# A four-layer graph kernel: the fp32r copy of the adjacency by a converting DMA of GpSimd in place of a ScalarE pass, with new orders

## Time and profile before

| | |
|---|---|
| median of three runs | 1117.52 us |
| the profiled execution, its own time | 1112.79 us |
| its span, first to last instruction | 1110.8 us |
| mean granted TensorE clock | 0.962 |
| HBM read / written | 38.61 MB / 4.19 MB |

### The profile page before, as it was taken

The page is one execution under the profiler, slowest core; times in us unless marked ns, Lnnn a source line. Parts: engine busy times, 40 slices in busy tenths (PEclk is TensorE's granted clock), DMA queues, the critical chain, the costliest instruction groups (busy, mean ns, idle before and its releaser), DMA issues.

```text
span 1110.8 us, 16047 instructions
## 1 busy us (share of the span) xinstructions
PE 961.9 (87%) x5024; PEld 616.0 (55%) x5024; DVE 945.3 (85%) x2710; ACT 885.8 (80%) x1876; POOL 97.7 (9%) x138
## 2 busy tenths in 40 slices
PE   4577897998989898998989898998989899898875
PEld 3354565656556565656556565656556565655442
DVE  4387889899898989989898999989898998988543
ACT  2378797979989797988989797988979798787643
POOL 1101010100101011010101010010101101000000
PEclk7569999999999999999999999999999999999989
DMA  2021102011111202011110201111110201101000
GB/s 88 10 76 48 39 11 86 11 39 49 48 48 35 61 11 70 27 39 48 48 48 10 86 11 44 43 48 49 48 48 10 85 2 40 48 1 48 1 10 9
DMA packets 34028, 43.92 MB, mean 40 GB/s; under 512 B 1040, under 2 KB 17424, under 8 KB 33936
## 3 DMA queue, kind: packets, MB, share of 16 engines
q1 hardware_dynamic: 25488, 38.61, 11.0%
q10 hardware_dynamic: 8448, 4.20, 1.3%
HBM read 38.61 MB, written 4.19 MB: 39 GB/s over the span
## 4 chain that ended last, share of the span: by engine, by line
PE 50%; DVE 32%; ACT 8%; issue 6%; POOL 3%; DMA 0%; DVEq 0%; ACTq 0%; POOLq 0%
DVE probs L604 8%; PE l_bank L865 7%; PE x_bank L949 5%; PE a_bank L894 5%; DVE probs L618 4%; DVE sess L774 3%; PE r_bank L1010 3%; DVE sess L767 3%; PE n_bank L1023 3%; ACT hn L368 3%; PE n_bank L1026 3%; PE a_bank L865 3%; PE n_bank L1010 2%; PE h_bank L1013 2%; PE l_bank L915 2%
## 5 line engine op out<-in xcount | busy, mean ns | idle before, releaser
L618 DVE SCALAR_TENSOR_TENSOR probs<-spread,s_lift,probs 128x512 f32<-128x512 f32 x320 | 232.9, 747 | 1.8
L604 DVE CUSTOM_DVE_ANT_0 probs<-spread,mask 128x512 f32<-128x512 f32 x320 | 211.9, 684 | 4.1 <-ACT spread L428 4.1
L444 ACT ACTIVATE pT<-l_bank 128x512 f32<-128x512 f32 x256 | 153.6, 600 | 40.7 <-PE l_bank L865 40.7
L436 ACT ACTIVATE probs<-probs,shift_p 128x512 f32<-128x512 f32 x256 | 184.7, 722 | 1.5 <-DVE probs L618 1.5
L865 PEld LDWEIGHTS l_bank<-ident,probs 128*128 128x128 f32 x1024 | 124.5, 144 | 79.0 <-issue 40.6
L865 PE MATMUL l_bank<-ident,probs 128*128 128x128 f32 x1024 | 155.9, 278 | 10.1 <-ACT probs L436 9.4
L350 POOL TENSOR_TENSOR rstd<-var_eps,power 128x4 f32<-128x4 f32 x64 | 74.1, 1158 | 967.1 <-DVE var_eps L598 641.6
L368 ACT ACTIVATE hn<-x,shift,rstd 128x128 f32<-128x128 f32 x192 | 79.4, 497 | 34.4 <-POOL shift L352 34.4
L915 PE MATMUL l_bank<-hT,dst_rep 128*128 128x512 f32 x128 | 71.9, 645 | 12.9 <-ACT pT L444 11.0
L428 ACT ACTIVATE spread<-l_bank 128x512 f32<-128x512 f32 x64 | 38.3, 599 | 41.9 <-PE l_bank L915 41.9
L996 PE MATMUL y_bank<-hn,sess 128*128 128x128 f32 x512 | 64.3, 279 | 8.2 <-DVE sess L774 8.2
(11 more groups left out here) (174 smaller groups left out, 2017.7 us busy)
## 6 DMA issues: line engine op xcount, KB each, us to landing
adj_i<-in_adj SPq DMA_DIRECT2D x16, 1024.0 KB, 5.1
adjt_i<-in_adj_t SPq DMA_DIRECT2D x16, 1024.0 KB, 5.5
xin<-in_x SPq DMA_DIRECT2D x16, 256.0 KB, 2.8
out<-out_sb ACTq DMA_DIRECT2D x16, 256.0 KB, 4.7
weights_sb<-in_weights SPq DMA_DIRECT2D x1, 840.0 KB, 4.4
```

Of the source, the lines that this page charges most:

```text
L436: s.activation(row, row, ACT.Exp, bias=shift_p[:, head, c:c + 1], accum_out=den[:, head, c:c + 1]).then_inc(probs_ready, 1)
L444: s.activation(pT[:, head - 1, :, c * P:(c + 1) * P], l_banks[unit % 2][:, :].rearrange("p (j i) -> p j i", j=C), ACT.Copy).then_inc(pT_co ...
L604: chain.link(v.tensor_tensor_reduce(out=row, in0=spread_row, in1=mask, scale=1.0 / LIFT, scalar=-3e38, op0=ALU.subtract, op1=ALU.max, accu ...
L618: v.scalar_tensor_tensor(row, spread_row, source, row, ALU.min, ALU.subtract, reverse1=True).then_inc(ready, 1)
```

## The change

The step edges is taken off ScalarE and put on GpSimd. There it is a DMA that reads adj (int32) from HBM again and writes it as fp32r into edges, with a semaphore for each buffer. The one user in the common case, TensorE's first agg of a graph, waits for the DMA's semaphore of its buffer. (VectorE's kinds step, in the way that is not taken here, then makes the values 0 or 1.) SyncE's load of the next adj_i no longer waits for edges. All of BEGIN and WHEN is replaced.

```diff
@@ BEGIN, WHEN: every number of the two tables is new @@
 BEGIN = (
-    (-21509, 8739, 15282, 21773, 28348, 34972, 41515, 48098, 54718, 61258, 67837, 74403, 80989, 87504, 94130,
-     100679),
...
+    (-5429, 20041, 26606, 33143, 39707, 46288, 52827, 59483, 66019, 72571, 79073, 85623, 92241, 98809, 105411,
+     111896),
...
@@ graph_layers @@
-        mask1_ready, count_ready, edges_ready = sem("mask1_ready"), sem("count_ready"), sem("edges_ready")
+        mask1_ready, count_ready = sem("mask1_ready"), sem("count_ready")
+        edges_loaded = [sem("edges_loaded0"), sem("edges_loaded1")]
@@ SyncE, load_adj @@
                     sp.wait_ge(mask1_ready, p.before().count(1, 1))
                     sp.wait_ge(count_ready, p.before().count(1, 1))
-                    sp.wait_ge(edges_ready, p.before().count(1, 1))
                 sp.dma_start(adj_i[:], rows(adj, p.graph)).then_inc(adj_loaded, 16)
@@ GpSimd, step_of @@
             def step_of(p, step):
+                if step == "edges":
+                    if p.before(2).exists():
+                        pool.wait_ge(agg_ready, p.before(2).count(LAYERS, LAYERS))
+                    g.dma_start(edges[:, p.graph % 2, :, :], rows(adj, p.graph)).then_inc(edges_loaded[p.graph % 2], 16)
                 if step[:5] == "stats":
                     deviation(p, int(step[5]))
@@ ScalarE, step_l @@
-                elif step == "edges":
-                    act.wait_ge(adj_loaded, p.count(16, 16))
-                    if p.before(2).exists():
-                        act.wait_ge(agg_ready, p.before(2).count(LAYERS, LAYERS))
-                    s.activation(edges[:, p.graph % 2, :, :], adj_i[:, :, :], ACT.Sign).then_inc(edges_ready, 1)
@@ VectorE, kinds (the way not taken) @@
-                        dve.wait_ge(edges_ready, p.count(1, 1))
+                        dve.wait_ge(edges_loaded[par], p.count_of_parity(16, 16))
@@ TensorE, agg @@
                     if layer == 0:
-                        pe.wait_ge(edges_ready, p.count(1, 1))
+                        pe.wait_ge(edges_loaded[par], p.count_of_parity(16, 16))
```

More of the change, by code:

```diff
@@ L41 @@
 BEGIN = (
-    (-21509, 8739, 15282, 21773, 28348, 34972, 41515, 48098, 54718, 61258, 67837, 74403, 80989, 87504, 94130,
-     100679),
[L44 to L49, removed]
+    (-5429, 20041, 26606, 33143, 39707, 46288, 52827, 59483, 66019, 72571, 79073, 85623, 92241, 98809, 105411,
+     111896),
+    (13526, 20049, 26553, 33166, 39703, 46305, 52896, 59433, 66037, 72495, 79063, 85666, 92240, 98820, 105362,
+     111953),
+    (13568, 20072, 26599, 33185, 39754, 46342, 52950, 59490, 66040, 72590, 79193, 85741, 92297, 98872, 105445,
+     112031),
+    (13546, 20068, 26667, 33223, 39788, 46390, 52950, 59524, 66016, 72579, 79189, 85731, 92330, 98847, 105476,
+     112046),
 )
```

## The result

The change took 1113.13 us (median of 20 runs, 1110.89 to 1117.25) against 1117.74 us (20 runs, 1112.52 to 1121.01): a ratio of 0.9967, with a 95% interval of 0.9954 to 0.9980. It is faster by 0.3%, some 4 us, where 11.1 us were forecast. The direction held and the size did not.

What follows compares the result with a forecast made beforehand. One loop was taken to bound it: VectorE from x2 to stats3, normalisation, TensorE from agg to x2. Over 12 periods at 0.8 us, -9.6, plus -1.5 filling, gave -11.1: 1106.4 us from 1117.5; own range 1097 to 1114, 8-in-10 range 1092 to 1123.

Steps and rivals of the forecast that it cites:

- The pass: ScalarE's edges pass, 1.900 us a graph, 30.4 us in all: off the loop, its removal costed at nothing in steady state.
- The issue: GpSimd's issue of each edges DMA, 0.37 to 2.41 us, between stats2 and stats3: hidden by idle time, costed at 0.
- the rival in which it keeps VectorE out: GpSimd's issue behind stats2 stops VectorE 1.01 or 2.41 us a graph: slower, 1122.6 to 1145.0 us; chance 0.13.
- VectorE's waits around x2: Waits for z_t and state_hi get smaller, a new one of 1 to 2 us for y_bank comes at x2.
- the filling of the pipeline: While the pipeline fills, the edges pass is on the chain; removing it gives -1.5 us.
- the term of x2: VectorE's x2 starts earlier, with mask1 filling the z_t wait and the state_hi wait gone: mean -1.15 us a period.
- g1_turn and src0: These VectorE steps now lie between x2 and stats3, costing 0.61 and 0.07 us: +0.68 us a period.
- values0 ahead of norm3: ScalarE does values0 in the 1.37 us it waited before norm3, bringing the split nearer: -0.40 us a period.
- First failed step: the clock: Periods at 0.97 take 64.3 and 64.6 us instead of 63.1; more or fewer move the time 1.3 us each, within range.
- The draining: The pipeline's end keeps its order of TensorE and VectorE work but for a few places: 0.
- It costs no more work (1.22 us either way), but fills the 1.09 us wait for z_t.: VectorE's mask1 ahead of g1_joint_r instead of behind mix; its price is n_t, count and avT 0.26 us later.
- Nothing gained: Removed waits come back elsewhere in the loop, both full engines keeping their work: 1117.5 us; chance 0.15.

Runs made afterwards that it cites:

- experiment 4: The kernel before with its old orders, edges by GpSimd's DMA in place of ScalarE's pass: 1116.74 us, 0.9999 (0.9975 to 1.0023).
- experiment 3: The changed kernel with the edges DMA issued for the first two graphs alone, later graphs reusing their adjacency: 1115.83 us, 0.9985 (0.9965 to 1.0006).
- experiment 9: The kernel before with one filling matmul, its result unread, ahead of rows3 on TensorE: 1109.83 us, 0.9955 (0.9934 to 0.9976).
- experiment 10: The changed kernel with two filling matmuls, their results unread, ahead of rows3 on TensorE: 1103.68 us, 0.9873 (0.9838 to 0.9907).
- experiment 1: The changed kernel with VectorE's src0 put back behind stats3: 1112.5 us, 0.9965 (0.9947 to 0.9983).
- 7: The kernel before with one move, mask1 directly behind stats1 on VectorE, no DMA on GpSimd: 1127.14 us, 1.0106 (1.0079 to 1.0134).
- 11: The changed kernel with mask1 behind the next graph's stats0 and two filling matmuls ahead of rows3: 1095.92 us, 0.9819 (0.9789 to 0.9849).
- experiment 12: The kernel of 11 with VectorE's max2 and src0 ahead of m0 behind stats3, and n7 ahead of x3: 1105.9 us, 0.9897 (0.9868 to 0.9926).

## Why the prediction was wrong in size

**What held.** The pass is worth nothing in steady state (experiment 4: 0.9999). The issue (0.81 us) and the landing (5.7 us) of the DMA cost nothing (experiment 3, and no wait of TensorE for edges). The issue lay between the 0.37 and 2.41 us given, and the rival in which it keeps VectorE out has no trace in 746 ns. The Trainium skill (DMA: Bandwidth & Descriptors, Anatomy of one DMA) gave an estimate of 4.4 us for the landing; the trace has 5.5 to 6.1 us for this converting transfer, so it takes a good microsecond longer than by that fit, to no effect here. VectorE's waits around x2 changed as said. For the filling of the pipeline, forecast at -1.5 us, experiments 9 and 10 have -1.2 us, but this shows nothing: up to the first split the profiled executions take 124.3 to 130.5 us, as the clock happens to be, so a term of this size can't be told.

Periods at full clock were forecast shorter by 0.87 us, taken as 0.8, and the pair of experiments 9 and 10 has 0.62 (62.48 against 63.10 us). That this is near was luck. The terms of the sum can be read in these two kernels (means of twelve graphs; x2 is its first instruction on VectorE, stats3 its var_eps, and the twelve graphs give 0.65 us a period):

| stretch and term | forecast | experiment 9 | experiment 10 | change |
|---|---|---|---|---|
| agg to the next x2: the term of x2 | -1.15 | 33.23 | 33.19 | -0.04 |
| x2 to stats3: g1_turn and src0 | +0.68 | 25.04 | 24.84 | -0.20 |
| stats3 to agg: values0 ahead of norm3 | -0.40 | 4.92 | 4.52 | -0.40 |

values0's term was right, with the mechanism given (norm3 no later, the split 0.4 us nearer). The term of x2 came to nothing, and the price of g1_turn and src0 was not paid: VectorE's busy time in that stretch grew by less than 0.1 us, so other steps had left it, which I had not looked for. Two errors cancelled.

**First failed step: the clock.** The sentence was: "More or fewer of them move the time by 1.3 us each, and this is in the range." I treated the clock as chance that both kernels share. It is not: it hangs on TensorE's waits at rows3, which the new orders changed. I had counted src0 ("+0.68", with g1_turn) as a cost of time alone. With s_lift ready earlier, values0's matmuls no longer wait, and two waits of TensorE of 1.43 us became one of 2.45 us. Nine periods of twelve have a clock of 0.97 in after's profile, two in before's. That the filling removes the falls is shown; that the joined wait makes them more frequent than the split one is likely but not shown, since experiment 1 did not split it, and the split waits of experiments 4 and 7 had falls in six and eight periods of twelve. Over the same thirteen graphs, filling TensorE's wait gives before 824.29 - 820.28 = 4.0 us and after 824.48 - 812.18 = 12.3 us, in the profiled runs. The two stretches without filling, of before and then of after:

```profile
192.02:1016.31 824.29, 749.85 (x4046) 481.86 (x4044) 755.58 (x2149) 710.62 (x1515) 75.26 (x102) 0.99 0.13 40
```

```profile
193.96:1018.44 824.48, 763.77 (x4047) 490.65 (x4047) 752.39 (x2152) 692.83 (x1502) 93.74 (x115) 0.98 0.19 57
```

The difference, 8.3 us, is as much as the 8.1 us that the new orders are worth there. By the medians it is milder, because before's other runs lose more than its profiled one and after's less: filling brings before 0.45% (5 us) and after 0.9% (10 us). So the clock took some 5 us of the forecast 11, and where it did not act, the change is worth 6 us (medians) to 9 us (ratios).

The draining was put at 0, and that failed by the same step: behind the last but one split, before's profile takes 56.03 us with a clock of 0.96 to the last split, after's 58.60 us with 0.91, and from there to the end they take 38.5 and 38.4 us. That is 2.5 us more.

**Second failed step: the term of x2, and mask1 in it.** The sentence was: "It costs no more work (1.22 us either way), but fills the 1.09 us wait for z_t." It costs VectorE nothing and GpSimd 0.9 us, on the path over norm1 to n_t, count and avT, which I had named myself as what is late next. I had avT 0.26 us later. Counted from agg, avT starts 0.78 us later (30.90 us behind it in experiment 9, 31.68 in 10), and 0.34 us later with mask1 moved (31.24 in 11; means of twelve graphs). From avT's start to x2 I had 1.25 us, and it is 1.51 us. TensorE did lose work from this stretch, as forecast, but it now spends the time won waiting for avT; of the whole change this was the rival "Nothing gained", and for this term it held. One such stretch, agg to x2, of the kernels of 9 and of 10; the second and third columns are its length and TensorE's busy time:

```profile
381.89:415.29 33.40, 33.33 (x191) 21.16 (x191) 30.21 (x81) 31.68 (x71) 2.78 (x4) 1.00 0.03 9
```

```profile
378.83:412.14 33.31, 32.59 (x187) 20.72 (x188) 29.93 (x82) 31.88 (x72) 3.69 (x4) 1.00 0.05 10
```

So -1.15 us was mis-sized by 1.1 us, of which mask1's place is 0.43 (with it moved, the stretch takes 32.76 us, -0.47). Moving mask1 is worth 0.44 us a period (experiments 10 and 11), 4 to 8 us in all. The Trainium skill (SBUF — State Buffer, Who interferes with whom) says that a VectorE operation that can enter a 2-port mode shuts GpSimd out for the whole instruction when it comes first, and that one with two SBUF inputs contends with GpSimd's reads. The runs agree in this case: mask1 began 0.17 us ahead and the rstd ended 0.9 us late, and the rstd beside m0 took 1.40 us, though the shift behind it got shorter by as much or more. The rule has two sides, and I used one. I priced GpSimd shutting out VectorE, and took VectorE's steady 740 to 753 ns as evidence that the two do not meet. The evidence was in the other engine's row: the longest rstd of before, 2.41 us beside a median of 1.007, stood in the earlier trace rows, and I used it as a bound and not as a sign; mask1 runs within it (156.77 to 157.99 us, the rstd from 155.62 to 158.03 us). Before even had the very pair while its pipeline filled, GpSimd first:

```profile
48.89 1.91 POOL L350 TENSOR_TENSOR rstd<-var_eps,power 128x4 f32<-128x4 f32 x1 [0.17 <-DVE var_eps L598]
...
48.72 1.22 DVE L670 TENSOR_SCALAR mask<-adj_i 128x2048 bf16<-128x2048 int32 x1
```

**Left open.** What about TensorE's waits brings the clock down was not measured beyond these cases: in after nine of twelve waits of 1.95 to 2.72 us had a fall behind them, and one of 2.39 us had none; the waits of 1.91 to 2.03 us in experiment 1 had one in seven cases of twelve; two waits with 1.6 us of matmuls between them (631.52 to 633.11 in before) had one in two, six and eight cases of twelve in before and experiments 4 and 7. The length of the wait does not decide alone. In experiment 9 only the wait for hn was filled and that for s_lift stayed (12.7 us in 11 cases, at most 1.4, in 205 to 900 us), and still the falls behind rows3 went. Why mask1's early place brings more falls in before was not settled either. No kernel was tried with mask1 at a place where GpSimd has nothing to do.

## What to carry to other kernels

When orders are changed, list the waits of TensorE by length and not by sum: a wait costs more than its length where the clock falls behind it, and a few matmuls without use in the gap are a cheap test for it (here they also pay). Check every term of a sum by its own stretch, since a total can be near by luck. When a large VectorE pass is moved, look at what GpSimd does at its new place; a GpSimd operation of 128 x 4 on the path to the next stage can wait for nearly all of it, and this is seen in GpSimd's durations, min, median and max, never in VectorE's. Look also at the operation behind it: a shorter rstd here only made the shift longer. Compare kernels by the same periods of the same graphs before summing up; here the three that kept the full clock were the short ones anyway.

## What the runs showed of the hardware

- An int32 to bf16 pass of VectorE (128 x 2048, 1.22 us) made a GpSimd tensor_tensor of 128 x 4 take 1.91 us instead of 1.01, in four kernels, with and without DMAs on GpSimd. VectorE's pass kept its 1.22 us.
- Nine waits of TensorE of 1.95 to 2.72 us, one in a period of some 63 us, were each followed by 3.4 us at 1.2 GHz, which made the period 1.2 us longer (the mean of nine, against the same periods with the wait filled). Three such waits were not followed by a fall, and their periods were equal within 0.02 us.
- Behind stats3, GpSimd's rstd and shift took 1.01 and 0.71 us in before, 1.39 and 0.24 us in after, and in experiment 12 again 1.03 and 0.68 us: about the same in sum.
- Two matmuls without use, 1.88 us of TensorE in each period of some 63 us, took 0.9% off after, in which TensorE is the busiest engine.
- A converting DMA of 1 MB (int32 to fp32r), issued by GpSimd in 0.81 us, landed in 5.5 to 6.1 us.
